# Sending and fetching the band of relative scores in two transfers by partition halves

## What is computed

```python
idx = jnp.arange(s)
dist = jnp.clip(idx[None, :] - idx[:, None], -R, R) + R      # R = 64
pe_k, pe_v = rel_emb_k[dist], rel_emb_v[dist]
...
score = jnp.einsum('bhqd,bhkd->bhqk', q, k) + jnp.einsum('bhqd,qkd->bhqk', q, pe_k)
attn = jax.nn.softmax(score, axis=-1)
ctx = jnp.einsum('bhqk,bhkd->bhqd', attn, v) + jnp.einsum('bhqk,qkd->bhqd', attn, pe_v)
```

## Time and profile before

| what | us |
|---|---|
| median of 3 runs (1685.96 to 1688.66) | 1687.14 |
| span of the profiled execution | 1677.5 |
| second attention, first L1407 to last work, about | 1102 to 1665 |

### The profile page before, as it was taken

The page is one execution under the profiler, slowest core; times in us unless marked ns, Lnnn a source line. Parts: engine busy times, 40 slices in busy tenths (PEclk is TensorE's granted clock), DMA queues, the critical chain, the costliest instruction groups (busy, mean ns, idle before and its releaser), DMA issues. The chain is left out here.

```text
span 1677.5 us, 38807 instructions
## 1 busy us (share of the span) xinstructions
PE 1552.2 (93%) x14424; PEld 1233.4 (74%) x14424; DVE 904.4 (54%) x3193; ACT 732.4 (44%) x1975; POOL 299.0 (18%) x376
## 2 busy tenths in 40 slices
PE   6899999999999999999599999959999999999996
PEld 5668888888888888888365656537777777777764
DVE  5336545454545454545322222237877777777774
ACT  2322222222222222222223232258888888888873
POOL 2010201111111101010430000003323332333232
PEclk9999999999999999999699999979999999999998
DMA  4009400000000000000243232258889998899886
GB/s 118 0 8 86 105 8 7 8 8 6 6 6 5 7 5 7 3 10 4 85 114 114 77 112 85 72 166 245 250 241 251 237 250 235 246 246 254 236 235 173
DMA packets 234032, 181.50 MB, mean 108 GB/s; under 512 B 82703, under 2 KB 223913, under 8 KB 233888
## 3 DMA queue, kind: packets, MB, share of 16 engines
q1 hardware_dynamic: 228514, 167.17, 37.1%
q0 software_dynamic: 5376, 12.44, 2.7%
HBM read 103.63 MB, written 75.78 MB: 107 GB/s over the span
## 5 line engine op out<-in xcount | busy, mean ns | idle before, releaser
L1547 ACT ACTIVATE a1Pm<-a1Pm,a1nmx 128x256 f32<-128x256 f32 x512 | 255.5, 504 | 0.4 <-DVE a1nmx L1609 0.3
L1609 DVE CUSTOM_DVE_ANT_0 a1Pm<-a1ps_S,a1Sb 128x256 f32<-128x256 f32 x512 | 196.1, 421 | 77.2 <-issue 75.5
L768 DVE TENSOR_TENSOR a0AT<-a0ps_AM,mask 128x384 f32<-128x384 f32 x256 | 125.5, 551 | 192.5 <-PE a0ps_AM L588 192.1
L773 DVE TENSOR_TENSOR a0MT<-a0ps_AM,mask 128x384 f32<-128x384 f32 x256 | 138.4, 555 | 88.2 <-PE a0ps_AM L609 85.1
L1542 ACT ACTIVATE a1Rt<-a1ps_R 128x384 f32<-128x384 f32 x264 | 128.6, 487 | 106.7 <-PE a1ps_R L1407 96.9
L1162 DVE TENSOR_TENSOR f1hid<-f1ge,f1ps_b 128x512 f32<-128x512 f32 x80 | 55.0, 688 | 192.1 <-PE f1ps_b L1095 182.4
L1426 PE MATMUL a1ps_T<-ident,a1Pm 128*128 128x128 f32 x1024 | 155.9, 275 | 0.0
L607 PE MATMUL a0ps_AM<-a0AT 128*128 128x256 f32 x512 | 152.9, 380 | 0.0
L572 PE MATMUL a0ps_qk<-xnT_all,a0w_in 128*128 (+1 forms) x512 | 138.3, 393 | 2.0 <-PEq L151 1.3
L715 ACT ACTIVATE a0qk<-a0ps_qk 128x512 f32<-128x512 f32 x128 | 76.4, 597 | 119.3 <-PE a0ps_qk L572 119.3
L1407 PE MATMUL a1ps_R<-rel_st,a1stk 72*128 72x192 bf16 x528 | 90.0, 253 | 35.5 <-ACT a1Rt L1542 13.2
(11 more groups left out here) (246 smaller groups left out, 2991.0 us busy)
## 6 DMA issues: line engine op xcount, KB each, us to landing
skew<-a1Rt SPq DMA_DIRECT2D x132, 384.0 KB, 5.4
a1Sb<-skew SPq DMA_DIRECT2D x131, 384.0 KB, 7.0
a1stk<-parts SPq DMA_DIRECT2D x153, 64.0 KB
a1stk<-parts SPq DMA_DIRECT2D x51, 192.0 KB
parts<-a1prt SPq DMA_DIRECT2D x18, 384.0 KB
f1w<-in_L_ffn_w_kernel SPq DMA_DIRECT2D x16, 344.0 KB
f1w<-in_L_ffn_w_kernel SPq DMA_DIRECT2D x16, 320.0 KB
f1wo<-in_L_ffn_wo_kernel SPq DMA_DIRECT2D x16, 320.0 KB
```

What stands on the lines that cost most here:

```text
L768: nc.vector.tensor_tensor(AT[i][h][:, :], ps_AM[i][h][:, 0:HB], mask[:, :], ALU.mult).then_inc(A_ready, 1)
L773: nc.vector.tensor_tensor(MT[i][h][:, :], ps_AM[i][h][:, 0:HB], mask[:, :], ALU.mult).then_inc(M_ready, 1)
L1547: nc.scalar.activation(Pm[:, place(h), :], Pm[:, place(h), :], ACT.Exp, bias=nmx[it][:, h:h + 1], scale=-1.0, accum_out=den[it][:, h:h + 1 ...
L1609: nc.vector.tensor_tensor_reduce(out=Pm[:, place(h), :], in0=ps_S[hp % 2][:, n, :], in1=bias_of(it, hp, n), scale=-1.0, scalar=3.0e38, op0 ...
```

## The change

A quarter of the band is sent and fetched in two transfers, one for partitions 0 to 63 and one for 64 to 127. One of the halves takes all 192 columns, the other the 128 columns that can reach its rows. Tiles 0 and 1 get places of their own in `a1Sb`, 448 columns in all, so the part that is cleared lies between them and is cleared by one memset. The semaphores count 32 for a quarter instead of 16. ScalarE, ahead of overwriting `a1Rt`, waits for the send of the tile before (`skew_out`) instead of its fetch (`skew_in`).

```diff
-        Sb = m.sb("a1Sb", [P, HP, 2 * REL + BAND, 2])
+        Sb = m.sb("a1Sb", [P, HP, T + BAND, 2])
...
-            c0 = REL * (1 - it)
+            c0 = BAND * it
             return Sb[:, hp, c0:c0 + T, n]
...
-                        act.wait_ge(skew_in[hp // PQ], s * 16)
+                        act.wait_ge(skew_out[hp // PQ], s * 32)
...
-                        v.wait_ge(skew_in[hp // PQ], (s + 1) * 16)
+                        v.wait_ge(skew_in[hp // PQ], (s + 1) * 32)
...
-                nc.vector.memset(Sb[:, :, 0:REL, :], 0.0)
-                nc.vector.memset(Sb[:, :, REL + BAND:2 * REL + BAND, :], 0.0).then_inc(sm["cleared"], 1)
+                nc.vector.memset(Sb[:, :, P:P + BAND, :], 0.0).then_inc(sm["cleared"], 1)
...
+                def halves(it):
+                    near, far = slice(0, P // 2), slice(P // 2, P)
+                    return ((near, P // 2, P), (far, 0, BAND)) if it == 0 else ((near, 0, BAND), (far, 0, P))
...
                     sp.wait_ge(sm["R_ready"], s * HP + (q + 1) * PQ)
-                    c0 = 0 if it == 0 else 2 * (P - 1)
-                    sp.dma_start(skew[it][:, ps, c0:c0 + 2 * BAND], Rt[:, ps, :, :].rearrange("p n c h -> p n (c h)")).then_inc(skew_out[q], 16)
+                    for rows, c, w in halves(it):
+                        to = 2 * (c + (0 if it == 0 else P - 1))
+                        sp.dma_start(skew[it][rows, ps, to:to + 2 * w], Rt[rows, ps, c:c + w, :].rearrange("p n c h -> p n (c h)")).then_inc(skew_out[q], 16)
...
-                    sp.wait_ge(skew_out[q], (s + 1) * 16)
+                    sp.wait_ge(skew_out[q], (s + 1) * 32)
                     flat = skew[it].rearrange("i n c -> (i n c)")
-                    sp.dma_start(Sb[:, ps, REL:REL + BAND, :].rearrange("p n c h -> p n (c h)"),
-                                 bass.AP(flat.tensor, flat.offset + 2 * (q * PQ * PITCH + P - 1),
-                                         [[2 * (HP * PITCH - 1), P], [2 * PITCH, PQ], [1, 2 * BAND]])).then_inc(skew_in[q], 16)
+                    for rows, _, w in halves(it):
+                        k = BAND - w if it == 1 else 0
+                        at = flat.offset + 2 * (q * PQ * PITCH + P - 1 + k) + rows.start * 2 * (HP * PITCH - 1)
+                        to = k if it == 0 else BAND + REL + k
+                        sp.dma_start(Sb[rows, ps, to:to + w, :].rearrange("p n c h -> p n (c h)"),
+                                     bass.AP(flat.tensor, at, [[2 * (HP * PITCH - 1), P // 2], [2 * PITCH, PQ], [1, 2 * w]])).then_inc(skew_in[q], 16)
```

More of the change, by code:

```diff
@@ L1795, in _ @@
                 for q in range(QUARTERS - 1):
-                    sp.wait_ge(skew_in[q], (2 * B + 1) * 16)
-                sp.wait_ge(skew_out[3], (2 * B + 1) * 16)
+                    sp.wait_ge(skew_in[q], (2 * B + 1) * 32)
+                sp.wait_ge(skew_out[3], (2 * B + 1) * 32)
 def store_stage(nc, x_all, out):
```

## The result

The changed kernel takes 1717.06 us in the median of 4 runs (1711.27 to 1718.41), beside 1686.55 us for the kernel before on the same chip (1682.36 to 1688.66). The ratio is 1.0186, with an interval of 1.0159 to 1.0213: 1.9% slower, about 31 us. The profiled execution has a span of 1716.5 us at a mean granted clock of 0.968 (before 1677.5 and 0.976).

A forecast was written before the change was run, and what follows sets the result against it. TensorE was taken as the bound at 33.37 us per sequence, DMA engines close behind. +0.9 and +0.45 us over 15 sequences gave +20, the start +1: span 1698.5, plus 9.6 gave 1708 us; forecast's own range 1697 to 1722, 8-in-10 range 1683 to 1765.

The forecast's parts named there:

- queries' loop: SP's queue in the second attention: extra issues delay the queries' last landing by +1.35, less room of 0.6: +0.75 us per sequence.
- the path of the fetch: The band fetch issued at 1255.65, which VectorE's first pair of heads awaits: +1.28 less 0.4 room, +0.9 us per sequence.
- The room of 0.4: Slack of the fetch issued at 1255.65: needed 6.91 us later, while the median fetch lands after 6.5.
- The issue cost: SP's time to issue one band transfer: 0.36 to 0.48 us, taken as 0.41, or 6.6 us more per sequence.
- Ahead of L1259: Before the split parts go out: the second quarter's later send and doubled fetch issue delay them by +0.6 us.
- the sum of SP's time: SP per sequence: 6.6 us of added issues fit as a sum into 13 us of waits.
- -0.3 and -0.15: Shorter band transfers queued ahead make the parts land 0.3 us and the last queries 0.15 us sooner.
- The half-height term: Band transfers of 64 partitions run slower: +0.43 us on each of two on the fetch's path, half showing, +0.45 per sequence.
- The first rival: DMA engines become the bound through slow half-height transfers: share above 0.92, period 36.3, 1734 us (1722 to 1806); chance 0.25.
- The second rival: Fewer bytes shorten landings by at least 1 us, the two delayed places vanish: -4.6 us, 1682.5 us; chance 0.20.
- The third rival: Landings in the second attention shorten by just what the extra issues cost: 1687 us, within 3; chance 0.15.
- the small parts: Longer clearing and doubled issues at the start: about +1 us once; ScalarE's earlier wait: nothing or a few tenths.

The follow-up runs named there:

- after_merged: The changed kernel with the first group of queries loaded in one transfer of 24 partitions instead of three of 8: 1689.19 us, ratio 1.0051.
- by_heads: The kernel before with each quarter of the band sent and fetched in two transfers of 128 partitions, one per pair of heads: 1709.21 us, ratio 1.0150.
- halves_full_width: The changed kernel with both partition halves taking all 192 columns, the bytes of before: 1740.9 us, ratio 1.0332.
- layout_only: The changed kernel with one transfer of 128 partitions and 192 columns per quarter each way: 1685.15 us, ratio 0.9992.
- narrow: The kernel before with one transfer of 160 columns per quarter, the last 32 of 192 left out from the third tile on: 1676.23 us, ratio 0.9942.
- send_halves: The changed kernel with only the sends by halves, each quarter fetched in one transfer of 128 partitions and 192 columns: 1702.11 us, ratio 1.0135.
- extra_issues: The kernel before with a tiny transfer of 64 partitions, 16 bytes each, behind every band send and fetch: 1777.65 us, ratio 1.0530.

## Why the prediction was right, and where it was not

- **Direction held, and so did the place: a loop through SP's queue.** The queries' loop sets the period, in every sequence, and TensorE waits at L1407 for `a1stk`. after_merged bears it out: take 1.6 us of issues out of that loop and 1.5 come back. by_heads bears out that the number of transfers costs by itself, 25 us.
- **The sum took the wrong one of its two paths.** It put the queries' loop at +0.75 us, dropped it, and counted +0.9 for the path of the fetch, for which VectorE waits. In the trace VectorE waits 9.1 us in 14 places for the band, 1.0 at most, and TensorE 33.6 us in 16 for the queries. The room of 0.4 on the fetch's path came from a median of 6.5 us that is the mean of two landings, 7.9 and 5.1, both of another quarter.
- **The issue cost was the mis-sized term.** I took 0.41 us, with 0.48 as the upper bound; the rows show 0.61 for 64 partitions. Four issues between the groups of queries were to cost +1.2, 8.1 us from the first to the third group; it became +3.96, 10.89 (+3.4 in the mean). The bound came from transfers of 128 partitions, while the nearest rows of another height, the queries with 2.08 for three of 8 partitions, would have given 0.69.
- **Ahead of L1259 I counted only the second quarter, +0.6.** It became +4.62 (+3.2 in the mean), because SP's backlog builds up over the whole step: 32 issues more or less back to back. To charge two places was too local; the sum of SP's time, which I found to fit (6.6 into 13 us), was really 13.2 into 13.2.
- **The landings of the parts and the queries became shorter, more than I took off.** -0.3 and -0.15 were -3.22 and -2.11 (in the mean -1.4, and -2.9 up to the next L1225). SP's waits fell from 13.2 to 4.9 us per sequence with it, which is why 13 us more of SP give only 2.65 us more of period. In halves_full_width, with the bytes of before, -0.7 and -2.3 are there already; the fewer bytes add -0.7 and -0.6.
- **The half-height term, +0.45, is not shown by any run.** By the pieces of the loop the landings of halves_full_width are no longer than those of by_heads; what half height cost shows in the time of the issues.
- **The period: 34.7 forecast, 36.02 measured;** +20 us of loop forecast, +34.5 measured against the same profiled execution and +26.0 against layout_only. The clock, left inside the range, took about 0.9 us of each sequence.
- **"The median lies 9.6 above the span" was wrong as a constant.** The changed kernel's span and median are 1716.5 and 1717.06, layout_only's 1686.1 and 1685.15. The 9.6 belonged to one quick execution, with fewer late sequences than most.
- **That 1717 fell into the range is in part luck.** From median to median 21 us were forecast and 30.5 came. The errors ran against each other: issues too cheap and counted in too few places, landings too long, the larger path not the one that counted, a term for half height that doesn't show. The total came out 9 us low because they nearly cancel.
- **The first rival's price was there in small part, its bound was not.** Half height does hold the engines longer, 1.15 times per byte where the rival's 1734 took about 1.5 (1.39 us for 320 KB against 1.11 for 384), but the share fell to 0.81 instead of rising above 0.92. Not the engines but SP's queue is nearly full: SP waits 4.9 us in 36.0.
- **The second rival's gain is real, and overpaid.** The parts and the queries land sooner, and narrow gains 10 us by fewer bytes. Against it stand 25 us for twice the transfers (by_heads).
- **The third rival** (all hidden) fell with by_heads. That the small parts cost nothing held for the layout and ScalarE's wait (layout_only). The start did not come out at +1: from the stage's first L1407 to the first L1225 it took 28.3 us before, 27.4 in layout_only and 32.1 after.

Beside each other, with bytes as before: twice the transfers +25 us, partition halves instead of heads another +31; a sixth fewer bytes then gives back 25. Alone, those bytes are worth 10.

What stays open: why the extra issues cost as much as they did, and why the halves take 0.61 us to issue when transfers of 24, 32, 96 and 128 partitions can take 0.3 to 0.4. The pieces of the loop come from one profiled execution of each kernel.

## What to carry to other kernels

Before a transfer is split, add up the issuing queue's time over the loop it sits in, with an issue time measured for that very shape, and see what other transfer of the same loop waits behind it. Here every byte saved was paid with an issue, and issues were the scarcer. Merging three small transfers into one on that queue gained 0.4% in the kernel before and 1.35% in the changed one.

## What the runs showed of the hardware

- The time SP needs to issue one transfer depends on its shape more than on its bytes, and for some on what was issued straight before. Medians over a run (and least values): 8 partitions 0.66 to 0.69 us (0.65), 24 partitions 0.32 to 0.48 (0.30), a mix of 32 and 96 0.45 (0.30), the halves of 64 partitions 0.61 (0.57 to 0.59), 128 partitions 0.36 to 0.47 (0.32 to 0.36), but 0.58 to 0.59 where a fetch of 128 stands behind transfers of 64 (send_halves, extra_issues). A transfer of 64 partitions with 16-byte pieces took 0.50 (0.46). Splitting by heads kept the issue at 0.44 us.
- A small transfer of 128 partitions with 16-byte pieces behind each band transfer, 16 per sequence, cost 7.8%, one with 64 partitions 5.3%, though they carry next to no bytes.
- Two transfers by partition halves held the engines 1.15 times as long per byte as two of all partitions; by 32 and 96 partitions it was (81.9 / 109.36) / (78.4 / 111.99) = 1.07.
